# Transformer and state-space block on one core: where the ones of the stacks are filled, two queues for the first stacking, and a new order table

## What is computed

```
x = x + 0.5 * ffn(norm(x));  x = x + mamba(norm(x));  x = x + 0.5 * ffn(norm(x))
ffn(x):   h = layernorm(x); h = causal 3-tap conv(h); q, k, v = h @ attn_w
          rotate q and k;  p = softmax(causal(q k^T / sqrt(8)))  (16 heads of 8)
          x = x + (p v) @ proj_w
          x = x + expert(argmax(layernorm(x) @ router))          (4 experts, 512 wide)
mamba(x): h = x + ssm(x) @ W_out;  h + silu(rmsnorm(h) @ w1 + b1) @ w2 + b2
```

## Time and profile before

| | |
|---|---|
| median of three runs | 1726.83 us (1722.39 to 1729.95) |
| profiled execution, device time | 1728.04 us |
| profiled execution, span from first to last instruction | 1725.9 us |
| TensorE matmul busy | 82% of the span |
| VectorE busy | 69% |
| ScalarE busy | 47% |
| GpSimd busy | 23% |
| mean granted TensorE clock | 0.890 of full |

### The profile page before, as it was taken

One profiled execution on the slowest core, in us unless ns is written; L12 is line 12 of the kernel. 1 busy time (PEld: TensorE's weight loads), 2 busy tenths in 40 slices (PEclk: granted clock), 3 DMA queues, 4 the chain that ended last, 5 costly groups with the idle time before them and its releaser, 6 DMA issues.

```text
span 1725.9 us, 30393 instructions
## 1 busy us (share of the span) xinstructions
PE 1412.1 (82%) x11328; PEld 742.7 (43%) x11328; DVE 1184.0 (69%) x2807; ACT 803.5 (47%) x1266; POOL 397.4 (23%) x404
## 2 busy tenths in 40 slices
PE   1477889859989999889989898899898986985846
PEld 0133434435444445454544454455544453443323
DVE  5657484588589767868688768887796657655622
ACT  0153443533646545544555455555454553552422
POOL 0102132123131331205031403133221422221110
PEclk9678886978989999899989998999999898997867
DMA  5221300021202021121203031203011003003000
GB/s 181 37 39 27 45 1 18 18 37 26 30 28 43 21 45 40 30 33 45 44 26 44 29 50 35 35 22 58 21 35 28 29 24 54 13 14 54 25 17 23
DMA packets 75807, 61.43 MB, mean 36 GB/s; under 512 B 6800, under 2 KB 71824, under 8 KB 75664
## 3 DMA queue, kind: packets, MB, share of 16 engines
q1 hardware_dynamic: 71568, 51.10, 15.7%
q0 software_dynamic: 4096, 8.40, 1.6%
HBM read 19.23 MB, written 14.55 MB: 20 GB/s over the span
## 4 chain that ended last, share of the span: by engine, by line
PE 29%; DVE 11%; issue 5%; DMA 3%; SPq 3%; ACT 2%; POOL 1%; POOLq 0%; DVEq 0%; ACTq 0%
PE wring L743 5%; PE wring L550 4%; PE wring L748 3%; PE obank L596 3%; SPq L465 2%; DVE mx L1282 2%; PE aring L611 2%; PE aring L636 1%; DMA stq<-shiftT 1%; PE aring L653 1%; PE aring L576 1%; PE wring L756 1%; DMA stk<-low 1%; PE wring L762 1%; PE wring L858 1%
## 5 line engine op out<-in xcount | busy, mean ns | idle before, releaser
L921 ACT ACTIVATE prob_mem<-aring 128x1024 f32<-128x1024 f32 x320 | 324.9, 1022 | 188.7 <-PE aring L653 172.4
L1282 DVE TENSOR_REDUCE mx<-aring 128x2 f32<-128x1024 f32 (+2 forms) x384 | 317.5, 862 | 116.9 <-PE aring L636 105.0
L743 PE MATMUL wring<-wv,hb 128*128 x448 | 241.2, 648 | 18.3 <-ACT hb L958 12.7
L611 PE MATMUL aring<-ramps,spots 64*128 64x128 bf16 (+1 forms) x2560 | 179.3, 220 | 67.1 <-DVE mx L1282 26.9
L596 PE MATMUL obank<-prob_mem,vx 128*9 128x512 f32 (+3 forms) x2048 | 196.4, 484 | 12.3 <-ACT prob_mem L921 6.0
L611 PEld LDWEIGHTS aring<-ramps,spots 64*128 64x128 bf16 x2560 | 84.9, 97 | 275.3 <-issue 154.1
L1393 DVE SCALAR_TENSOR_TENSOR yv<-yv,wring 128x512 f32<-128x512 f32 x112 | 76.8, 685 | 110.2 <-ACT yv L963 109.6
L653 PE MATMUL aring<-stq,stk 50*128 50x512 bf16 (+3 forms) x1024 | 135.7, 325 | 0.0
L636 PE MATMUL aring<-stk,stq 48*128 48x512 bf16 (+3 forms) x1024 | 132.4, 320 | 0.0
L748 PEld LDWEIGHTS wring<-ep,yaT 128*128 128x128 f32 x896 | 112.6, 192 | 42.6 <-issue 42.0
L748 PE MATMUL wring<-ep,yaT 128*128 x896 | 125.6, 283 | 5.4 <-ACT yaT L873 5.0
(11 more groups left out here) (212 smaller groups left out, 2354.7 us busy)
## 6 DMA issues: line engine op xcount, KB each, us to landing
hb<-hd SPq DMA_DIRECT2D x16, 448.0 KB
stq<-high SPq DMA_DIRECT2D x96, 64.0 KB
stk<-high SPq DMA_DIRECT2D x96, 64.0 KB
stq<-mid SPq DMA_DIRECT2D x64, 64.0 KB
stk<-mid SPq DMA_DIRECT2D x64, 64.0 KB
od<-ob SPq DMA_DIRECT2D x16, 256.0 KB, 2.3
od<-ob SPq DMA_DIRECT2D x16, 192.0 KB, 2.1
x<-in_x SPq DMA_DIRECT2D x8, 256.0 KB
```

The lines of the kernel that those rows point to most:

```text
L611: pe.matmul(dst, spots[rows, 2 * by_key + part, :], ramp, start=(part == 0), stop=False, skip_group_check=True)
L743: last = pe.matmul(ring[:], hTd[:, u * P:(u + 1) * P], wv[:, expert[u], o:o + DFF], start=True, stop=True)
L921: act.activation(prob_mem[:, k], ring[:], ACT.Exp, scale=float(HD) ** -0.5).then_inc(freed, 1)
L1282: last = dve.tensor_reduce(mx[:, j, h0 + q:h0 + q + 3:2], ring[:, :, c:c + w], AX_X, ALU.max)
```

## The change

Five edits, shown below: (1) the ones are filled by GpSimd, at the end of its setup, over all 128 partitions and 4096 elements of both `stk` tensors (two instructions in place of VectorE's four), and whoever stacks waits for a new semaphore `setup_ones`; (2) row 0 of x is loaded ahead of the constants; (3) of block 0's stacking the 12 DMAs of the keys are issued by ScalarE, between its own copies, and the 12 of the queries stay with SyncE; (4) rows 2 to 4 of x are loaded after block 0's stacking, row 1 where rows 1 to 4 were; (5) `ORDER` is another string of the same length with the same number of each digit.

```diff
@@ ORDER (first two lines of 18; the others are replaced too)
-    "00000000000000111111111111111101011111111111110111111111011101001111112111212121202221016101111111140110141404"
-    "44444444444144144444414544414414115111111151111511333333333333131131133131323113231321331233323311321321123131"
+    "00000000000011111110101110111110111111111111011110111111111111111011021121212121021122011110106011141144414144"
+    "41441014444414444444440454414144111151111510511333333333133113113312333112332323133233313231233312131131161"
...
@@ @block.sync
-            for dst, src in loads:
-                sp.dma_start(dst[:], src).then_inc(s["const_loaded"], 16)
...
-                        for side in range(2):
+                        for side in range(2 if n > 0 else 1):
                             sp.wait_ge(ready, 2 * n + side + 1)
                             for product in (Q_ROWS, K_ROWS)[side][which]:
                                 stack(side, piece, product)
+                    if kind == "low" and n == 0:
+                        for later in range(2, XROWS):
+                            sp.wait_ge(s["x_loaded"], 16 * later)
+                            load(later)
...
             load(0)
+            for dst, src in loads:
+                sp.dma_start(dst[:], src).then_inc(s["const_loaded"], 16)
...
-            for row in range(1, XROWS):
-                sp.wait_ge(s["x_loaded"], 16 * row)
-                load(row)
+            sp.wait_ge(s["x_loaded"], 16)
+            load(1)
+            sp.wait_ge(s["setup_ones"], 2)
@@ @block.scalar
+            def stack_keys(piece, which):
+
+                for product in K_ROWS[which]:
+                    for a in range(2):
+                        first = HALF * a + HD * product
+                        act.dma_start(stk[0][1][first:first + HD, :, :],
+                                      piece[1][HALF * a:HALF * a + HALF, :]).then_inc(s["a_stacked"], 16)
...
+                        if n == 0:
+                            act.wait_ge(s["setup_ones"], 2)
+                            act.wait_ge(s["a_high"], 2)
+                            stack_keys(high, 0)
...
+                        if n == 0:
+                            act.wait_ge(s["a_mid_copied"], 2)
+                            stack_keys(midl, 1)
+                    elif kind == "low" and n == 0:
+                        act.wait_ge(s["a_low"], 2)
+                        stack_keys(low, 2)
@@ @block.gpsimd
+            pool.wait_ge(s["setup_rank"], EXPERTS - 1 + UNITS)
+            for k in range(2):
+                pool.memset(stk[k][1][:].rearrange("p h t -> p (h t)"), 1.0).then_inc(s["setup_ones"], 1)
@@ @block.vector
-            for a in range(2):
-                for k in range(2):
-                    step(dve.memset(stk[k][1][HALF * a + 32:HALF * (a + 1)], 1.0))
-
```

More of the change, by code:

```diff
@@ L158 @@
 ORDER = (
-    "00000000000000111111111111111101011111111111110111111111011101001111112111212121202221016101111111140110141404"
-    "44444444444144144444414544414414115111111151111511333333333333131131133131323113231321331233323311321321123131"
-    "11611111131313414144441444444114444434444441344444414151151531133131313153130013133130131310310030303202303203"
-    "23303311313131333123332311321132103601311011300313141141141111441134411114114311114441143411140441113144111444"
-    "14244514412441114225331131521230251303216303331130313131031110403111441444441041143414114131443111141400313441"
@@ L164 @@
[L164 to L173, removed]
@@ L174 @@
-    "43245243422353325323025303230363333003030033043444444444334344413444114444441314444131441411315311133111311131"
-    "13311113331131111113131511311111311531131532323223323232026000000004444444444444444441111414141441411411414144"
-    "1514115111511111111151111111111111111112222222264444444444444444444444544444444555"
+    "00000000000011111110101110111110111111111111011110111111111111111011121121212121021122011110106011141144414144"
+    "41441014444414444444440454414144111111151511110511333333333133113113312333112332323133233313231233312131131161"
@@ new lines @@
+    "13111314144114441444144441144344414441344544444411413115133133553331131131330313033331031111303113303001303333"
+    "31003233323303232032312023211313130311130316131131143111440311144114414041114441144114114114411401144441401444"
+    "01114045114100115111125532123031211233333320323133123133311333133311613310113113331114134141144111444411444411"
+    "14134414144110104041114014111441135123241124120412311321314124120101061311031515331131313411134041114411441441"
+    "11444114544411104441001141411142414414415244141221505211115213132033123331133331131161310310333413313333101014"
@@ new lines @@
+    "34111311333311114431144141104440111414111423114244214244444121102323120341154411414641113001114541144311415444"
+    "14444411440404114344541141144404111531441443143331315153101115131121321123301213133333322133213333121133313033"
+    "31100106311131013341111341144401144114441140411411444114444011014401114414111321412412431112323020311321310532"
+    "01343133331113411111161141410541104544110144114411411444411404411104541114111144512441124424244512150101001101"
+    "52323113233101133333311311311161133441334113341131031143411311434114444111040441434411331411144413321142442441"
@@ new lines @@
+    "21230213214231131005436114151131154101410441114443144441431514414411411434111144444151441411044331114511151323"
+    "11313151322113130332333301333223312333012313033033331113331113116011114331414410141141103411144134410143111441"
+    "11441411213112444142441214412441314124311512431512156311111311131331111111344414514414414144411444444101141411"
+    "04110444442424242425050022050250333333333363433441433343431313313134431413443331431141141144314114311111441411"
+    "14441411411111451111441145311131511113323232325233332323026000000044044444444444414414114444144114144511414114"
@@ L177 @@
+    "1141111111111551111511111111111111111112222222264444444444444444444444544444444555"
 )
@@ L376, in build_program @@
             setup_chain const_loaded attn_w_loaded weights_loaded setup_weights setup_pool
-            setup_dve setup_act setup_dve2 setup_rank x_loaded out_stored a_link c_link b_link
+            setup_dve setup_ones setup_act setup_dve2 setup_rank x_loaded out_stored a_link c_link b_link
             a_mid_copied a_u a_var a_rstd a_hn a_cT a_rope a_high a_mid a_low a_stacked a_shift a_shiftT
@@ L1563, in _ @@
             step(dve.tensor_scalar(v("b1", 0, 4), v("b1", 0, 4), 0.5, None, ALU.mult))
-            dve.wait_ge(s["setup_chain"], sc)
-            for a in range(2):
-                for k in range(2):
-                    step(dve.memset(stk[k][1][HALF * a + 32:HALF * (a + 1)], 1.0))
             dve.wait_ge(s["setup_act"], 1)
```

## The result

The changed kernel takes 1780.99 us (median of four runs, 1767.36 to 1781.42), the kernel before 1728.39 in the same comparison (1722.39 to 1733.06): a ratio of 1.0287 [1.0228, 1.0346], so slower by about 50 us, where 1708 had been forecast. Its profiled execution took 1780.83 us, with a span of 1778.9 and a mean granted clock of 0.873 (0.890 before).

What follows compares the result with a forecast made beforehand. TensorE (82% busy) and VectorE (69%) were taken to bound the middle, one serial chain the start. Terms -16.2 - 3.0 + 4.0 - 4.0 = -19.2 us took 1728.04 to 1708.8, or 1708 in median terms; range 1695 to 1722.

Steps and rivals of the forecast that it cites:

- The fills leave VectorE, x ahead: Start chain: fills save 17.2 us, x ahead costs 0.7, memory sharing 0.3; net gain 16.2 us (14.3 to 16.8).
- slow fill: Rival, GpSimd setup: fills take 25.2 us each, time 1747; begins to matter at 5.5 us a fill; chance 0.05.
- Two engines on one memory side: Setup: GpSimd's second fill slows VectorE's three casts by about 0.1 us each, 0.3 in all; ends 0 and 2.0.
- The stacking from two queues: Block 0's stacking: two issuing queues bring core 0's first product 3.0 us earlier, between 0 and 9.5.
- the engines bound the stacks: Rival, block 0's stacking: the same 8 of 16 engines serve both queues, no gain; time 1711; chance 0.22.
- Front 1's products: Behind core 0's sixth and seventh max step: products and rotation lose their cover, costing 4.0 us (0 to 9.6).
- The table elsewhere: Rest of the order table: same work, only waits change; 6 gained, 2 lost, net -4 us (-12 to +10).
- given back: Rival: stacks gain nothing, front 1's products are serial, table costs 2; about 1722, no measurable change; chance 0.16.
- the issue bounds them: Rival, block 0's stacking: stacks land 2 us behind the last issue, front 1's products fit gaps; about 1700; chance 0.12.
- a first product later than 51: Sign of a wrong forecast: core 0's first score product after 51 us, where 44 to 50.5 was expected.
- a start that gains: Sign of a wrong forecast: start gains 19 us, time does not follow; blames the table, seen as lower TensorE busy shares.

Runs made afterwards that it cites:

- e3: Kernel before with only the ones' fills moved from VectorE to GpSimd; 1709.05 us, 0.9867.
- e15: e5 with rows 1 to 4 of x loaded ahead of block 0's stacking; 1716.85 us, 0.9923.
- e1: The changed kernel with the old order table, all other edits kept; 1717.97 us, 0.9933.
- e5: e1 with all 24 DMAs of block 0's stacking on SyncE; 1707.61 us, 0.9877.
- e4: Kernel before with only block 0's 12 key stacking DMAs issued by ScalarE; 1736.56 us, 1.0031.
- e9: e5 with SyncE waiting for all six pieces of block 0 before its first stacking issue; 1721.2 us, 0.9931.
- e8: Kernel before with only the first 64 digits of the order table new, then the old table's; 1745.55 us, 1.008.
- e2: Kernel before with the whole new order table and nothing else of the change; 1796.91 us, 1.036.
- e10: e5 with at most four of block 0's stacking DMAs in flight; 1715.14 us, 0.9892.
- e11: Kernel before with 184 random swaps of neighbouring core, state-space and expert digits in the old table; 1805.93 us, 1.0415.

## Why the prediction was wrong

**The fills leave VectorE, x ahead: right.** 16.2 us forecast, 16.0 measured. The fills took 3.5 us each (6.96 / 2), not the 4.2 carried over from the f32 fill, and only VectorE's casts waited for them (next paragraph): GpSimd was idle 4.18 us ahead of its first power. The constants landed 0.76 us later (9.04 against 8.28), as forecast. No slow fill came near 5.5.

**Two engines on one memory side: the size right, the mechanism not.** The first bfloat16 cast took 0.78 us in the changed kernel (from 9.12), 2.23 in e3 (from 7.67) and 0.45 in e15 (from 9.46), and in all three it ended at 9.90 or 9.91, just behind the fills' end at 9.8. It was held until the fill was over, and so was the scaling of `negA` just ahead of it (0.79 us, where it took 0.17 before). This is the Trainium skill's rule (SBUF — State Buffer, "Who interferes with whom"), which I had set below the rows of shorter instructions; the trace agrees with it. In e3 VectorE's chain begins 1.45 us earlier, at 7.59, and gains nothing from it: its statistics start at 11.88, against 11.80. In the changed kernel the hold cost 0.5 us (from the landing of the constants to the cast of `spots` 1.57 us instead of 1.07), where 0.3 was forecast, only because the fills ended earlier than I had them end.

**The stacking from two queues: wrong sign.** Forecast -3.0, with 0 as the upper end. From the first issue to the first product it took 26.6 us (26.1 in e1) where one queue took 22.7 before and 23.9 in e5. In whole times e4, the direct comparison, puts it at +5 (1 to 10), and e1 against e5 at +10 (0 to 20). The rival "the engines bound the stacks" is nearer: the Trainium skill's "Issuing engines are not separate DMA queues" (DMA: Bandwidth & Descriptors) allows for no gain but issue time, and the runs go further, to a small loss: in the mean packets took 127 to 130 ns in e1 and the changed kernel, 116 in e5. That two queues lengthen packets isn't shown beyond this, as e9's one queue gave 127 too. I had no term for a loss, since I bounded a concurrency by 0 on its bad side. The other part of the gain, ahead of the stacks, stayed: the first product at 54.38 is 12.1 us earlier.

**Front 1's products: right.** +4.0 forecast, 3.5 to 5.4 measured: so far do e8 and e2, in which only the table is new, lag behind before from the 280th to the 440th matmul, and in the same stretch the changed kernel comes 3.7 to 6.5 us behind e1. e8's 14 us in the whole time are no measure of this term, since some 10 of them arise at the join of its two tables, which the new table does not have.

**The table elsewhere: the step that failed.** Forecast -4 with +10 as the upper end; e2 puts the whole table at +62 to +67 and e1 against the changed kernel at +61. Less the 4 to 5 of front 1's products, about +57 is this term, more than five times its end. The reasoning was "the work is the same; only waits can change", and then I looked only at the two waits that DMAs end. Those did improve (16.5 to 9.9 behind the maxima, and 6.0 to 2.3 behind the stacks). Both halves of the argument missed: the waits behind VectorE, which I took for fixed, rose (`mx` 25.0 to 43.8, `u` 6.0 to 20.3), and the same work took TensorE 32 us longer, with a granted clock of 0.88 instead of 0.94 from 400 to 800 us and 0.94 instead of 0.96 from 800 to 1200. In the profiled executions the clock stood at 1.2 GHz, the lower of its two levels, for 381 us before, 453 after, 368 in e1 and 463 in e2: the lower clock goes with the new table. Why it falls there is open. The distance in digits between `low` and the first max step, by which I had valued the table, says nothing of the waits that rose.

**The sum.** By ratios over about 1730 us, each from its own run: fills and x ahead -21 (e5), second queue +10 (e1 less e5), table +62 (e2), together +51 against +50 measured. The first two make e1's -12 by construction; what the sum tests is that the table costs the same in the old kernel and in the changed one. e5 and e15, nearly the same kernel, lie 8 us apart by their ratios, so the second queue's share is uncertain by as much as it is large. The rival "given back" stood 15 us above the forecast and still below before; the measured time stands 73 above it. In the rival "the issue bounds them" the sum takes 2 us off for front 1's products, where fitting them into gaps would take off the whole 4.0; nothing hangs on it. Of the named signs of a wrong forecast two came about: a first product later than 51 (54.38), and a start that gains (12.1 us, not 19) with a time that doesn't follow, which rightly put the blame on the table. It was to be seen in lower busy shares of TensorE, and these hardly fell (356.77 of 400 us against 359.93 from 400 us on): what fell is the number of matmuls in the same busy time.

## What to carry to other kernels

An order table of in-order engines is not neutral when it holds the same work: here 90 swaps of neighbours cost 29 us, so a new table must be priced as an unknown, as large as its disturbance (none of the reordered tables tried here was faster than the old one), and measured by itself (with the old one in the new kernel, too). A table joined from two has a price of its own at the join: lay it beside both parents at equal matmul counts before giving its time to a part. The safe part of such a change is the part that shortens one visible chain: moving the fills alone gives 0.9867 and should be taken with the old table and one queue. Look at the granted clock of a stretch, not only at waits, before calling TensorE's busy time constant.

## What the hardware showed that was not expected

- Two queues gave no gain for small pieces: 25.1 to 26.6 us from first issue to first product for 24 pieces of 64 KB from two, 18.4 to 25.9 from one. Packets of 1 KB between the same partitions took 58 to 186 ns (means of 64), and 67 to 130 ns in the mean of a kernel, in kernels that stack the same pieces. What sets it is open.
- The product's wait was not shortened by holding pieces back: with at most four in flight (e10) packets took 82 ns in the mean, and the whole 25.9 us.
- A GpSimd fill holds a cast of VectorE to the fill's end, however early the cast starts: 2.23 us from 7.67, 0.78 from 9.12, 0.45 from 9.46.
- ScalarE needed 0.80 us for an issue (4.77 / 6), SyncE 0.69 (4.11 / 6).
- TensorE's granted clock differs with the order of the same work: 0.94 and 0.96 over 400 to 800 and 800 to 1200 us before, 0.88 and 0.94 after, 0.92 and 0.94 in e11. It does not simply follow TensorE's idle time: e11 has more of that than the changed kernel (364 us against 335) and the higher mean clock (0.886 against 0.873 in the profiled executions).
